# Three engines' steady steps written out one after another instead of loops over two steps

## What is computed

```python
def reference(x, itok, ctx_2048, g_xattn, g_ffn, Wr, br, Wd, bd, Wu, bu):
    # first block: expert e = min(itok // 6250, 3); Wg = Wu = Wd = ctx_2048[e]
    h = layernorm(x)
    a = h @ W[e].T
    y = (silu(a) * a) @ W[e].T
    x = x + tanh(g_xattn) * y
    # second block: top 2 of 8 experts, rank 16
    h = layernorm(x)
    gates = softmax(h @ Wr + br + bonus); w = normalised top-2 gates
    hid = relu(h @ Wd[e] + bd[e])
    x = x + tanh(g_ffn) * sum_e w[e] * (hid[e] @ Wu[e] + bu[e])
```

## Time and profile before

| | |
|---|---|
| time, median of three runs | 202.97 us (202.61 to 202.98) |
| span of the profiled execution (first to last instruction) | 201.4 us |
| median less that span | 1.57 us |
| PE busy | 175.0 us, 87% |
| DVE busy | 155.7 us, 77% |
| ACT busy | 111.9 us, 56% |
| POOL busy | 99.7 us, 50% |
| mean granted TensorE clock | 0.974 |

### The profile page before, as it was taken

One profiled execution on the slowest core, in us unless ns is written; L12 is line 12 of the kernel. 1 busy time (PEld: TensorE's weight loads), 2 busy tenths in 40 slices (PEclk: granted clock), 3 DMA queues, 4 the chain that ended last, 5 costly groups with the idle time before them and its releaser, 6 DMA issues.

```text
span 201.4 us, 4382 instructions
## 1 busy us (share of the span) xinstructions
PE 175.0 (87%) x1074; PEld 104.0 (52%) x1075; DVE 155.7 (77%) x523; ACT 111.9 (56%) x224; POOL 99.7 (50%) x246
## 2 busy tenths in 40 slices
PE   1576896999997989999999999999999999976560
PEld 1564463655553656656656556655665655534310
DVE  4859696697768799889888998797877878678640
ACT  2596599884287166473665726547265561545200
POOL 4478846427246366375553735516244162445641
PEclk9999999999999999999999999999999999999955
DMA  5947572101210201203101011011010100101121
GB/s 135 370 163 231 205 216 69 52 5 20 86 55 0 52 0 52 59 0 104 55 0 54 0 52 52 2 52 52 0 54 0 52 20 33 52 0 55 52 104 52
DMA packets 6784, 13.43 MB, mean 67 GB/s; under 512 B 2392, under 2 KB 2520, under 8 KB 6768
## 3 DMA queue, kind: packets, MB, share of 16 engines
q0 software_dynamic: 2560, 8.39, 12.6%
q1 hardware_dynamic: 4208, 4.86, 7.3%
HBM read 9.06 MB, written 4.19 MB: 66 GB/s over the span
## 4 chain that ended last, share of the span: by engine, by line
PE 44%; issue 18%; POOL 10%; DVE 9%; DMA 7%; ACT 4%; DVEq 3%; SPq 2%; POOLq 1%; ACTq 0%
PE ps_y L603 6%; PE ps_y L605 6%; PE ps_y L604 6%; PE ps_a L603 4%; PE ps_a L605 4%; PE ps_a L604 4%; DMA xs<-in_x_dram,rows_of 4%; ACT h L796 3%; POOL rs L457 3%; PE ps_h2T L685 2%; PE ps_pT L624 2%; DMA bu_nat<-in_L_ffn_bu_dram 2%; POOL hot_slot L432 2%; PE ps_hT L677 2%; POOL xs L439 2%
## 5 line engine op out<-in xcount | busy, mean ns | idle before, releaser
L456 POOL TENSOR_SCALAR ve<-mv 128x1 f32<-128x1 f32 x32 | 7.7, 239 | 62.6 <-DVE mv L1099 51.8
L796 ACT ACTIVATE h<-xs,mrs,rs 128x512 f32<-128x512 f32 (+1 forms) x16 | 21.1, 1317 | 22.4 <-POOL mrs L458 22.4
L783 ACT ACTIVATE pT_hi<-ps_pT 128x512 f16<-128x512 f32 x19 | 11.3, 595 | 36.0 <-PE ps_pT L624 36.0
L603 PE MATMUL ps_y<-w_hi,pT_hi 128*128 x76 | 28.8, 379 | 2.3 <-DVE w_lo L952 1.5
L603 PE MATMUL ps_a<-w_hi,hT_hi 128*128 x76 | 29.1, 382 | 0.7 <-DVE hT_lo L1074 0.6
L604 PE MATMUL ps_a<-w_lo,hT_hi 128*128 x76 | 29.1, 382 | 0.0
L605 PE MATMUL ps_a<-w_hi,hT_lo 128*128 x76 | 29.0, 381 | 0.0
L604 PE MATMUL ps_y<-w_lo,pT_hi 128*128 x76 | 28.8, 379 | 0.0
L605 PE MATMUL ps_y<-w_hi,pT_lo 128*128 x76 | 28.8, 379 | 0.0
L1086 DVE SCALAR_TENSOR_TENSOR xs<-ps_y,y_t,xs 128x512 f32 x19 | 14.3, 750 | 10.2 <-PE ps_y L605 7.7
L529 POOL DMA_INDIRECT out_dram<-xs,rows_of x16 | 17.3, 1083 | 5.9 <-DVE xs L1117 3.5
(11 more groups left out here) (209 smaller groups left out, 424.0 us busy)
## 6 DMA issues: line engine op xcount, KB each, us to landing
w_nat<-in_ctx_dram SPq DMA_DIRECT2D x4, 1024.0 KB, 7.9
xs<-in_x_dram,rows_of POOLq DMA_INDIRECT x16, 3.6
wd_nat<-in_L_ffn_Wd_dram SPq DMA_DIRECT2D x1, 256.0 KB
wu_nat<-in_L_ffn_Wu_dram SPq DMA_DIRECT2D x1, 256.0 KB
out_dram<-xs,rows_of POOLq DMA_INDIRECT x16, 2.9
b_in<-in_L_ffn_bd_dram SPq DMA_DIRECT2D x1, 64.0 KB
bu_nat<-in_L_ffn_bu_dram SPq DMA_DIRECT2D x3, 16.0 KB
tok_i<-in_itok_BxS_dram SPq DMA_DIRECT2D x1, 8.0 KB, 1.8
```

The lines of the kernel that those rows point to most:

```text
L603: mm(ps[:, :], lhs_hi[:, kc, :], hi, start=(kc == 0), stop=False)
L796: a(h2[:, :, :], x1[:, col(k), :].rearrange("p o (q c) -> p c (o q)", c=KC), ACT.Identity, bias=mrs[:, 1, col(k)], scale=rs[:, 1, col(k)]) ...
```

## The change

`pipeline` no longer looks for like steps. It calls `step(i, i)` for every step with a plain number, on TensorE, ScalarE and VectorE, so that no loop, no counter and no expression of a counter is left.

```diff
         def pipeline(eng, step, first, pairs, tiles):
 
-            def work(i):
-
-                return ([(some(NP, off, i), i + off == 0) for off in pairs]
-                        + [(some(T, off, i), i + off == 0) for off in tiles])
-
             end = max(NP - min(pairs), T - min(tiles))
-            while first < end:
-                last = first + 1
-                while last < end and work(last) == work(first):
-                    last += 1
-                if last == first + 1:
-                    step(first, first)
-                else:
-                    odd = (last - first) % 2
-                    if odd:
-                        step(first, first)
-                    with eng.Fori(0, (last - first) // 2) as n:
-                        step(n * 2 + (first + odd), first)
-                        step(n * 2 + (first + odd + 1), first)
-                first = last
+            for i in range(first, end):
+                step(i, i)
```

## The result

The changed kernel takes **200.18 us**, median of four runs (199.56 to 201.85), against 202.79 us (202.55 to 202.98, four runs) for the kernel before beside it. The ratio is 0.9887, 95% interval 0.9839 to 0.9936. A few executions of either kernel run more than 1.5% above its fastest; the ratios leave them out, the medians do not. The profiled execution of the changed kernel took 200.31 us, with a span of 198.6 us against 201.4.

A forecast was written before the change was run, and what follows sets the result against it. The second layer norm's ring, 8.58 us a turn, was taken to hold TensorE above its 8.29 us floor. Gains of 1.45 (steps 10 to 17) and 0.40 (step 18), 1.85 us off 202.97, gave 201.12 us, range 200.6 to 202.9.

The forecast's parts named there:

- The bound and steps 10 to 17: TensorE waits for `h2` in its loop steps; without register work each takes 8.29 us, gaining 1.45 us (1.05 to 1.45).
- The pieces of the ring: Second layer norm's turn, `h2` through VectorE and GpSimd to the next `h2`: 8.58 us in loops, 8.04 written out.
- Step 18: TensorE's written-out step waiting for an `h2` that comes through VectorE's last loop step: gain 0.40 us (0.23 to 0.50).
- Jumps: Idle time at loop jumps back, 0.30 us on VectorE and 0.39 on TensorE, already inside the 1.45 us.
- The branch half of the rule on instruction fetch: A taken branch whose target has left the buffer makes the engine wait for a fetch; read as not holding for TensorE.
- Instruction supply: About 4 more code packets for TensorE's written-out steps, 0 to 5.6 us in all, taken as 0.
- slower supply: Rival, chance 0.11: TensorE's 4 further code packets are exposed at 1.4 us each, giving 206.7 us.
- hidden register work: Rival, chance 0.10: queues already hid register instructions, the ring stays near 8.5 us, giving 202.6 to 202.9 us.
- half the gain: Rival, chance 0.11: the ring drops below 8.29 us only in some steps, gaining 0.7 to 1.0 us.
- the beginning: Steps up to 7, same instructions in both kernels: no change, within 0.1 us either way.
- the end: From step 19 on, a line of waits without loops: moves earlier as a whole and keeps its length.
- The 1.57: Difference in us between the three runs' median, 202.97, and the profiled span, 201.4; taken as unchanged.

The follow-up runs named there:

- the second run: The changed kernel timed again without any edit, five rounds, beside the kernel before: 201.19 us against 203.32, ratio 0.9911 (0.9890 to 0.9932).

## Why the prediction was right and wrong

**The bound and steps 10 to 17: right.** The floor of 8.29 us and the loss of 1.45 us above it were read correctly; 1.46 came back. That the register work of the ring made the loss is now shown from both sides: VectorE and ScalarE written out give all of it with TensorE in loops, and a ring made longer by 0.39 and 0.76 us takes TensorE's step with it.

**The pieces of the ring: the sum right, the parts not.** 8.58 to 8.04 was read from two turns; the ring's own length is 7.98. And 8.58 is only one of the loop's turns: a body is two steps, and the turn after the one in the earlier trace rows, from 120.59 to the 129.02 of the earlier trace rows, is 8.43. The turns go on 8.58, 8.44, 8.58, 8.43, with 1.60 and 1.53 us from `ve` to `h2` in turn. That 8.58 matched the 8.57 us of an average step in steps 10 to 13 was luck:

```profile
100.45:125.99 25.54, 25.46 (x166) 14.91 (x164) 22.75 (x76) 14.13 (x27) 13.21 (x36) 1.00 0.08 31
125.99:134.71 8.72, 8.58 (x58) 4.96 (x55) 7.03 (x22) 4.69 (x9) 3.33 (x9) 1.00 0.08 31
```

Steps 10 to 12 take 8.51 each, the mean of the two turns, and step 13 takes 8.72 because TensorE's jump is in it. For the loads ahead of `add_y` I had 0.11 us a turn. That nearly held in VectorE's first loop (3.42 to 3.51 us from `w8` to `add_y` against 3.35, 0.12 on average); in its second loop they cost 0.32. The forecast did not depend on it, since TensorE's floor cuts the gain, but a forecast for ScalarE alone would have: by my pieces the ring would have been 8.58 - 0.29 = 8.29 everywhere, and it was 8.46 to 8.61 in the second loop.

**Step 18: right, slightly small.** 0.40 (0.23 to 0.50) against 0.46. Most of the idle time ahead of `add_y` went, and with it the 0.12 ahead of the statistics.

**Jumps: right in effect.** They were inside the 1.45. That one of them was most of what TensorE alone gave back, and that all four cost TensorE 0.02 us when the other two engines are written out, was not foreseen. The branch half of the rule on instruction fetch, in the Trainium skill's page "Runtime: NRT & Kernel Launch", section "Instruction fetch mechanics", is not seen at TensorE's jumps: with its loops kept and the ring out of the way, 0.02 us over four jumps leave no wait that a fetch could fill.

**Instruction supply: right.** Ten packets instead of six, as forecast, and no gap beside them: from 76 to 168 us six of the ten arrive, about one in two steps, and every one of steps 7 to 17 takes 8.28 or 8.29 us. The kernel with TensorE alone written out has the ten packets too, and measures 1.0020 (0.9986 to 1.0054). The rivals of slower supply, of hidden register work and of half the gain fall with this and with the steps at 8.29 us.

**What failed: two terms put at nothing.** The sum in the span was 1.85 us, and the named steps gave 1.92. The time still came out 0.9 us lower than forecast, for these reasons:

- "I put them at nothing, within 0.1 us either way", on the beginning, and the like for the end. The work there is indeed the same, and on average nothing changes that the runs can show. But a profile is one execution: the landing in step 1 and the fall of the clock in the last outputs moved it by 0.66 and 0.22 us, and between the fourteen profiles the end alone differs by up to 1.2 us. Predicted span 199.55, less 0.07 for the steps, 0.66 and 0.22, is the measured 198.6 us; with 1.71 us around it, 0.14 more than was put there, that is the profiled execution's 200.31. Forecasting the average was right; the allowance of 0.1 and 0.2 us for it was too small for a median of a few runs. The same kernel, timed again with 12 executions, gave a median of 201.19 us, inside the range, and a ratio of 0.9911, where 201.12 / 202.97 of the forecast is 0.9909. That agreement to 0.0002 is luck in part: the interval of 0.9890 to 0.9932 allows gains from 1.4 to 2.2 us, and the forecast's 1.85 us were all in the span, where the mean gain below is 1.71 inside it and 0.39 around it.
- "The three runs' median, 202.97 us, stands 1.57 us above that span, and I leave this difference as it is". Both halves were wrong. The 1.57 sets a median beside the span of another execution; within one execution the kernel before has 2.14 us around its span. And this time did not stay: it fell by 0.39 us with VectorE's code. Over 31 and 11 executions the mean span fell from 201.06 to 199.35 us, 1.71, and the time around it from 2.14 to 1.75, 0.39; together 2.1 us, which is the 203.32 - 201.19 of the medians. A fifth of the gain is in a place that no view of the profile shows. Counted in, it would have put the forecast at 200.7 us and the low end of the range at 200.2, beside the measured 200.18.

So the mechanism and its size in the steps were right, and the range was wrong on its lower side. The lowest case by the forecast's own terms is 202.97 - 1.95 - 0.1 - 0.2 = 200.72 us, which it rounds to 200.8, and the range stopped 0.1 us below that, with nothing held for parts that the span doesn't contain. Why the time around the span fell stays open.

## What to carry to other kernels

When several engines pass work around in a ring, add up one turn, of every step of a loop's body, and compare it with the busiest engine's step: what is over it is the most that any edit of the ring can give, and edits on different engines don't add beyond it. Register work costs where it carries a wait or stands between a wait and the work, on the engines of the ring; on the engine that is the bound it cost 0.34 us beside the loops of the other two and 0.02 us without them. For a kernel whose expected change is 1%, pair each time with the span of the same execution, and hold half a microsecond for landings at the beginning and the clock at the end before a range is called narrow.

## What the runs showed of the hardware

- The time around the span goes with the program and is steady: 2.10 to 2.21 us over the executions of the kernel before beside the second run, 1.71 to 1.78 for the changed one. It took one of two values, some 0.4 us apart, with VectorE's code; neither the presence of one loop (1.78 us) nor the number of TensorE's packets (ten with 2.16 us, six with 1.76) decides it.
- TensorE's jump back, which showed 0.39 us of idle time in the earlier trace rows, cost 0.02 us over four jumps when VectorE and ScalarE had no loops (steps 7 to 17 in 91.20 us against 91.18).
- An activation of one element adds 0.10 us to ScalarE's queue (8 of them 0.76 us), though it is recorded as longer: two show 0.30 us, and `h2` begins 0.20 us after the first.
- The moment at which the clock falls at the end differs between executions of one kernel and sorts the fourteen profiles: 24.39 to 24.49 us from step 19 on when the last output begins at the upper clock, 25.20 to 25.57 when it begins at the lower.
- VectorE's wait for a landing in step 1 ended at 31.24 and at 31.78 us in two executions of the changed kernel, and step 7 began 0.53 us later in the second.
